# VectorE sums the squares of q and k right behind their rope products, and ACT makes the rsqrt seeds ahead of the copy of O

## The reference

```python
x = x + _L0_attn_a_ref(_layernorm(x), ...)   # causal attention, 16 heads, polymax
x = x + _L0_ffn_ref(_layernorm(x), ...)      # 6 layers, below
x = x + _L0_attn_b_ref(_layernorm(x), ...)   # causal attention, softmax
x = x + _L0_ffn_ref(_layernorm(x), ...)      # the same 6 layers again
```

```python
def attn_layer(x, Wqkv, qs, ksc, Wo):
    q, k, v = split(x @ Wqkv)
    q = l2norm(q) * qs                  # t / max(|t|, 1e-12), head by head
    k = l2norm(k) * ksc
    q = q * cos * scale + rotate_half(q) * sin * scale
    k = k * cos * inv + rotate_half(k) * sin * inv
    out = local_attention(q, k, v)      # windows of 32, each sees itself and the one before
    return out @ Wo
for i in range(DEPTH):
    x = attn_layer(shift_tokens(x), ...) + x
    x = ffn_layer(shift_tokens(x), ...) + x
```

## Time and profile before

| | |
|---|---|
| median of 3 runs | 4362.58 us (4357.62 to 4364.63) |
| profiled execution, its own time | 4365.13 us |
| its span | 4363.3 us |
| TensorE busy | 3866.2 us (89%) |
| VectorE busy | 3296.5 us (76%) |
| ACT busy | 2534.1 us (58%) |
| POOL busy | 2498.8 us (57%) |

### The profile page before, as it was taken

One profiled execution on the slowest core, in us unless ns is written; L12 is line 12 of the kernel. 1 busy time (PEld: TensorE's weight loads), 2 busy tenths in 40 slices (PEclk: granted clock), 3 DMA queues, 4 the chain that ended last, 5 costly groups with the idle time before them and its releaser, 6 DMA issues. The chain is left out here.

```text
span 4363.3 us, 151598 instructions
## 1 busy us (share of the span) xinstructions
PE 3866.2 (89%) x66488; PEld 2314.4 (53%) x66488; DVE 3296.5 (76%) x4385; ACT 2534.1 (58%) x3236; POOL 2498.8 (57%) x2036
## 2 busy tenths in 40 slices
PE   6887799999999999999778877899999999999997
PEld 3323456665665666665433334566666666666664
DVE  7997777888888787888454436788888878878884
ACT  6885456566665666666324444556566565666654
POOL 0001677777777777777100005786777777777773
PEclk8999999999999999999789998999999999999998
DMA  0001232332323233222000002323323223232221
GB/s 19 1 1 42 72 87 65 85 77 75 83 67 87 73 78 85 62 67 62 17 1 1 1 14 74 92 62 84 81 67 85 73 79 80 73 81 71 66 60 40
DMA packets 165593, 260.83 MB, mean 60 GB/s; under 512 B 58572, under 2 KB 79816, under 8 KB 164936
## 3 DMA queue, kind: packets, MB, share of 16 engines
q1 hardware_dynamic: 164936, 251.13, 22.2%
HBM read 48.61 MB, written 1.05 MB: 11 GB/s over the span
## 5 line engine op out<-in xcount | busy, mean ns | idle before, releaser
L1374 POOL TENSOR_TENSOR f_k_rotated<-f_rope_ak,f_rope_bk 128x1024 f32<-128x1024 f32 x192 | 454.5, 2367 | 288.7 <-DVE f_rope_bk L1429 288.7
L1097 PE MATMUL banks<-f_wqkv,H 128*128 128x512 f32 x1152 | 564.9, 614 | 17.4 <-DVE f_E L1469 9.2
L1097 PE MATMUL banks<-f_wqkv,G 128*128 128x512 f32 x1152 | 551.8, 601 | 0.0
L1426 DVE TENSOR_TENSOR f_rope_aq<-banks,f_rope 128x1024 f32<-128x1024 f32 x192 | 235.1, 1225 | 389.5 <-ACT f_sqq L1284 376.2
L1361 POOL MEMSET f_kT<- 128x256 f32 x2 | 0.6, 311 | 839.9 <-POOLq L514 460.5
L1374 POOL TENSOR_TENSOR f_q_rotated<-f_rope_aq,f_rope_bq 128x1024 f32<-128x1024 f32 x192 | 454.5, 2367 | 29.0 <-DVE f_rope_bq L1429 28.6
L1319 ACT ACTIVATE f_V<-banks 128x1024 f32<-128x1024 f32 x192 | 196.8, 1025 | 418.7 <-PE banks L1097 418.3
L1152 PEld LDWEIGHTS banks<-f_O_T,f_wo 128*128 128x128 f32 x3072 | 372.6, 192 | 98.3 <-issue 94.6
L1152 PE MATMUL banks<-f_O_T,f_wo 128*128 128x128 f32 x3072 | 375.4, 275 | 6.4 <-issue 5.2
L1392 POOL TENSOR_TENSOR f_E<-f_E,f_row_inverse 128x1024 f32<-128x1024 f32 x192 | 368.6, 1920 | 19.8 <-DVE f_row_inverse L1484 19.8
L1386 POOL TENSOR_TENSOR f_q_rotated<-f_q_rotated,f_inverse_norm 128x1024 f32<-128x1024 f32 x192 | 365.2, 1902 | 15.0
(11 more groups left out here) (207 smaller groups left out, 8961.6 us busy)
## 6 DMA issues: line engine op xcount, KB each, us to landing
f_P_T_paired<-f_P_T SPq DMA_DIRECT2D x1536, 64.0 KB
f_V_previous<-f_V SPq DMA_DIRECT2D x192, 384.0 KB, 3.7
f_V_previous<-f_V SPq DMA_DIRECT2D x192, 128.0 KB, 2.4
f_wqkv<-in_L_ffn_Wqkv SPq DMA_DIRECT2D x48, 384.0 KB, 4.1
f_rope<-in_rope SPq DMA_DIRECT2D x24, 512.0 KB, 5.1
f_wo<-in_L_ffn_Wo SPq DMA_DIRECT2D x12, 512.0 KB, 5.4
f_w<-in_L_ffn_W SPq DMA_DIRECT2D x12, 341.0 KB
f_w<-in_L_ffn_W SPq DMA_DIRECT2D x24, 64.0 KB
```

What stands on the lines that cost most here:

```text
L1097: mm = nc.tensor.matmul(ps[:, o * BLK:(o + 1) * BLK], xs, w[:, c * INNER + o * BLK:c * INNER + (o + 1) * BLK], start=True, stop=True)
L1374: nc.gpsimd.tensor_tensor(qk[i][:], ra[i][:], rb[i][:], ALU.add).then_inc(radd.sem, 1)
L1426: nc.vector.tensor_tensor(heads_of(ra[i][:]), src, table(2 * i, 0, DH), ALU.mult).then_inc(rot.sem, 1)
```

## The change

On VectorE, the sum of q's squares moves behind the rope products of q, and the sum of k's squares and the clamp move behind the rope products of k, ahead of maximum and subtraction. On ACT, the two seed instructions move from behind the exponential of E to behind the copy of V, ahead of the copy of O. The waits move with them.

```diff
@@ ACT @@
                 if feed(s, 11) is not None:
                     nc.scalar.preload_act_table_set("natural_log_exp_and_others")
+                if live(s):
+                    act.wait_ge(clamped.sem, clamped.at(n))
+                    act.wait_ge(newton.sem, newton.past(n - 1))
+                    nc.scalar.activation(lg[:], ss[n % 2][:], ACT.Ln).then_inc(seeded.sem, 1)
+                    act.wait_ge(seeded.sem, seeded.at(n, 1))
+                    nc.scalar.activation(y0[:], lg[:], ACT.Exp, scale=-0.5).then_inc(seeded.sem, 1)
                 if live(s - 3):
                     act.wait_ge(o_mm.sem, o_mm.at(n - 3))
...
                     nc.scalar.activation(E[(n - 1) % 2][:], E[(n - 1) % 2][:], ACT.Exp).then_inc(expd.sem, 1)
-                if live(s):
-                    act.wait_ge(clamped.sem, clamped.at(n))
-                    act.wait_ge(newton.sem, newton.past(n - 1))
-                    nc.scalar.activation(lg[:], ss[n % 2][:], ACT.Ln).then_inc(seeded.sem, 1)
-                    act.wait_ge(seeded.sem, seeded.at(n, 1))
-                    nc.scalar.activation(y0[:], lg[:], ACT.Exp, scale=-0.5).then_inc(seeded.sem, 1)
@@ VectorE @@
                 if live(s):
                     rotate(s, 0, q_mm, PQ)
+                    sums(n, 0)
                 if live(s - 2):
...
                 if live(s):
                     rotate(s, 1, k_mm, PK)
+                    sums(n, 1)
+                    dve.wait_ge(red.sem, red.at(n))
+                    nc.vector.tensor_scalar(ss[n % 2][:], ss[n % 2][:], 1e-24, None, ALU.max).then_inc(clamped.sem, 1)
                 if live(s - 1):
...
-                if live(s):
-                    sums(n, 0)
-                    sums(n, 1)
-                    dve.wait_ge(red.sem, red.at(n))
-                    nc.vector.tensor_scalar(ss[n % 2][:], ss[n % 2][:], 1e-24, None, ALU.max).then_inc(clamped.sem, 1)
```

## The result

| | before | after |
|---|---|---|
| median of 4 runs | 4363.6 us (4357.62 to 4365.05) | 4799.14 us (4783.87 to 4818.95) |
| profiled execution: own time, span | 4365.13, 4363.3 us | 4783.87, 4782.1 us |
| TensorE busy | 3866.2 us (89%) | 4027.5 us (84%) |
| mean granted clock of TensorE | 0.974 | 0.931 |

The ratio is 1.1004, 95% interval 1.0962 to 1.1045. The forecast was 4620 us, with a range of 4575 to 4720. The sign was right; the time lies 79 us above the range.

What follows compares the result with a forecast made beforehand. The prediction took POOL's wait for the rsqrt seed, 476.6 us, as the sign of the loop setting the slot. Profiled 4365.1 + 237 (longer second loop, blocked clamp) + 20 (clock falls) = 4622, so 4620 us as median; range 4575 to 4720.

Steps and rivals of the forecast that it cites:

- Step (1): POOL's seed loop loses maximum, subtraction and q sum: 17.05 to 13.5 us, at least about 14 by POOL's order.
- Step (2): Loop between successive `f_rope_aq` through `out` becomes the late one; 10.77 us to the end of subtraction if the clamp isn't blocked.
- Step (3): On VectorE, the moved clamp waits for POOL's k sum of products: 1.16 us more per slot, +237 us for both calls.
- Step (4): ACT's seeds ahead of the copy of O cost nothing; without cover, the copy's 1.0 us a slot.
- Step (5): The first twelve slots, with little or no FFN work, change by 0 us, bounds -10 and +10 for both calls.
- Step (6): TensorE's longer gap lets its clock fall to 1.2 GHz, some 1.8 us each: +20 us, bounds 0 and +150.
- I allow 12 of them: Allowance for falls of TensorE's clock to 1.2 GHz behind longer gaps: 12 falls, +20 us.
- the clock falls in most slots: Rival: longer gaps drop TensorE's clock, 1.8 us for each of 166 slots on top of 4600, about 4900 us; chance 0.12.
- case of half the slots: Milder case of the rival on TensorE's clock: it falls in half of the slots, 4750 us.
- clamp not blocked: Rival: VectorE's moved clamp doesn't wait for POOL; 4388 us; chance 0.06.
- faster: Rival: TensorE becomes the bound, about 4197 us, if `f_rope_aq` to subtraction's end is under some 9.7 us; chance 0.04.

Runs made afterwards that it cites:

- experiments 1: Changed kernel with the clamp instruction left out, the seeds waiting for the two sums: 4378.75 us, 1.0043.
- Experiment 4: Changed kernel with a wait added so that POOL's k sum of products starts only when the clamp is done: 4431.47 us, 1.0163.
- experiment 6: VectorE's part of the change alone, ACT's seeds staying behind the exponential of E as in the kernel before: 4721.74 us, 1.0835.
- experiment 7: ACT's part of the change alone on the kernel before, VectorE in its old order: 4781.66 us, 1.0963.
- experiment 2: Changed kernel with six filler products of 128x512 on TensorE ahead of its wait for the subtraction: 4616.98 us, 1.0585.
- experiment 5: Changed kernel with POOL's k sum of products waiting for the clamp, plus three filler products on TensorE: 4409.72 us, 1.0112.
- experiment 8: Kernel before with only the q sum moved behind q's rope products; k sum, clamp and seeds stay: 4304.97 us, 0.9869.
- experiment 9: Kernel before with the q sum moved behind q's rope products and E's transpose moved behind the clamp: 4352.39 us, 0.9978.

## Why the prediction was right in its parts and wrong in its time

- **Step (1), the old loop**: held. POOL's wait for the seed fell from 476.6 to 122.6 us.
- **Step (2), the second loop**: held. `out` waits for `f_E`; with the block taken away the end of subtraction comes 10.5 to 10.7 us after `f_rope_aq` (experiments 1 and 4; forecast 10.77).
- **Step (3), the clamp behind POOL**: held, 1.31 us in all 192 tiles (1.30 to 1.33) and 11.86 us to the end of subtraction (forecast 11.93). The rule in the Trainium skill, "SBUF — State Buffer", section Who interferes with whom, says that whoever issues first holds the shared ports for its whole instruction, and that `tensor_reduce` never contends on trn2. The trace agrees: the two moved sums keep their 1.21 and 1.20 us, the second one over POOL's running product, and of the moved instructions only the clamp waits. Experiment 4 changes who is first, and the clamp is back at 0.18.
- **Step (4), ACT's seeds at no cost**: held for the length of a slot without falls (the cover was there), but not for the clock: experiment 6, without this part, is 77 us faster than the change. And experiment 7 shows the price without it, far above the 1.0 us a slot that the step named (421 us, falls included): not only the copy of O but the exponential too was behind the seeds.
- **Step (5), the first twelve slots, 0 with bounds of 10**: missed. They took 10 us more in experiment 2 and 41 more in the change; the 31 between them go when TensorE's gap is filled.
- **Step (6), the clock, is the step that failed.** It had the gaps nearly right (2.2 us in C and about 3 in B; medians 2.33 and 2.58 measured) and the price of a fall too (1.8 us; 152 / 103 = 1.5 measured). It failed in "I allow 12 of them": there were 103. Spans make the account without any count: before 4363.3; without the clamp 4373.6 (+10); clamp blocked, TensorE kept busy 4606.6 (+233); the change 4782.1 (+175.5). 20 us were allowed for the last term. The +233 holds more than the block: with the clamp in its place but free of POOL, and no falls, the span is 4414.0 (experiment 5), so some 40 are the clamp's own (31 by the medians) and some 193 its wait.
- What misled was the argument against the rival "the clock falls in most slots": that the clock was 1.00 before with gaps in every slot, and that TensorE stays some 85% busy. Those gaps were shorter (0.86 us in the earlier trace rows, at most 1.16 us in slots 12 to 95), and the mean busy share doesn't tell how often the clock falls: TensorE is busy for 87.2% of the first call's slots in experiment 6 and for 87.5% in the change, with 9 falls there and 56 here. The rival itself was well priced: 103 times 1.8 on 4600 is 4785, though 1.8 is too much for a fall and the first twelve slots are not in it. Its chance of 0.12 was too small, and the range should have reached to its case of half the slots, 4750, and beyond.
- **The rivals "clamp not blocked" and "faster"** are out. The point from which the second was to decide, 9.7 us to the end of subtraction, is supported by experiment 8: at 9.4 to 10.0 us (medians by slot) the kernel is faster than before, though only by 56 us.

What stays open: why the clock falls in some slots and not in others with the same gap (34 falls in 42 slots B of the change, 22 in 40 slots D), and what the filler changes for the clock, the length of the gap or the work ahead of it, which were not varied apart; and whether the meeting of `f_xn` with POOL is what costs experiment 9 its gain, which is read from the trace and not tested.

## What to carry to other kernels

When a loop is shortened, write down the next one with all that the change puts into it, and look at every small instruction in it that would run into a product of POOL: it can take over the product's remaining time, as the clamp did here and `f_xn` in experiment 9 (the k sum did not), and it may be cheaper to let the neighbour wait for it (here a wait added on POOL took 368 us away). Then ask what the new waits do to TensorE's clock: where a wait makes one gap in each slot longer, price the falls for most slots, not for a few, and test it with idle products that fill the gap.

## What the runs showed of the hardware that was not expected

TensorE's granted clock fell to 1.2 GHz 103 times in 166 slots with one gap of 2.3 to 2.6 us each (medians by slot), though the engine was busy for 88% of the first call's slots (1425.25 of 1628.50 us). Six small products in the gap, 1.46 us of work that nothing needs, removed all falls and made the kernel 182 us faster; two removed about half. And one VectorE instruction of 0.18 us, on 32 numbers a partition, cost 409 us of span by its place (4782.1 - 4373.6): some 40 by standing there at all (4414.0 - 4373.6), 193 by its wait of 1.13 us for POOL's product in each of 192 tiles (4606.6 - 4414.0), 175.5 through the clock.
